# Attention on one core: both halves of a product side by side in every second step, and the two maxima matmuls of a step side by side

## The reference, cut to what matters

```
e1 = prelu(w1 @ x + b1)          # 32 x 1024 for each image
e2 = prelu(w2 @ x + b2)
asm = prelu(wa @ x + ba)         # 64 x 1024, the values
score = softmax(e1^T @ e2, axis=2)        # 1024 x 1024 for each image
out = asm @ score^T
```

## Time and profile before

| what | value |
|---|---|
| median of 3 runs | 803.87 us (802.46 to 804.47) |
| the profiled execution | 805.25 us |
| its span, first to last instruction | 803.4 us |
| TensorE matmuls busy | 690.5 us, 86% of the span |
| VectorE, GpSimd, ScalarE busy | 583.7, 424.3, 409.9 us |
| mean granted TensorE clock | 0.947 of full speed |
| attentions | from 356 to about 711 us of the span |

### The profile page before, as it was taken

The page is one execution under the profiler, slowest core; times in us unless marked ns, Lnnn a source line. Parts: engine busy times, 40 slices in busy tenths (PEclk is TensorE's granted clock), DMA queues, the critical chain, the costliest instruction groups (busy, mean ns, idle before and its releaser), DMA issues.

```text
span 803.4 us, 9141 instructions
## 1 busy us (share of the span) xinstructions
PE 690.5 (86%) x2570; PEld 350.8 (44%) x2570; DVE 583.7 (73%) x899; ACT 409.9 (51%) x709; POOL 424.3 (53%) x254
## 2 busy tenths in 40 slices
PE   4777888875499998979999999989999999866887
PEld 2332332321377775744334343333434343225883
DVE  7996999996314337876768687876868687798746
ACT  2486888984101013016464655646474656554570
POOL 5447778783512133013959587692959497632000
PEclk9898999998599999988999999999999999987899
DMA  7000000000000003032003030302102030000005
GB/s 303 0 0 1 0 0 0 0 0 1 1 0 0 0 1 78 1 79 65 14 7 74 1 80 0 80 2 52 27 11 68 0 79 1 0 1 0 1 2 209
DMA packets 8105, 24.90 MB, mean 31 GB/s; under 512 B 2048, under 2 KB 2176, under 8 KB 7936
## 3 DMA queue, kind: packets, MB, share of 16 engines
q1 hardware_dynamic: 8064, 24.45, 11.1%
HBM read 6.09 MB, written 4.19 MB: 13 GB/s over the span
## 4 chain that ended last, share of the span: by engine, by line
PE 50%; DVE 26%; issue 12%; ACT 5%; POOL 4%; DMA 1%; SPq 1%; DVEq 0%; POOLq 0%; ACTq 0%
PE PS L1415 13%; PE PS L1492 10%; PE PS L1459 7%; PE PS L1481 4%; DVE SM L625 3%; DVE RB L402 3%; PE PS L1440 3%; PE PS L1450 2%; DVE RB L477 1%; DVE PS L469 1%; PE PS L1626 1%; PE PS L1422 1%; PE PS L1654 1%; DVE RB L484 1%; DVE SM L382 1%
## 5 line engine op out<-in xcount | busy, mean ns | idle before, releaser
L625 DVE TENSOR_REDUCE SM<-PS 128x1 f32<-128x512 f32 x256 | 172.8, 686 | 80.1 <-PE PS L1459 75.7
L1006 ACT ACTIVATE RB<-PS 128x512 f32<-128x512 f32 x256 | 139.2, 599 | 107.6 <-PE PS L1481 103.4
L1231 POOL TENSOR_TENSOR RB<-RB 128x1024 f32<-128x1024 f32 x66 | 156.2, 2385 | 20.7 <-ACT RB L1006 12.3
L1459 PE MATMUL PS<-R 96*128 96x512 f32 x256 | 123.0, 481 | 12.9 <-DVE SM L625 9.2
L1415 PE MATMUL PS<-R,WS 128*128 128x512 f32 x432 | 119.7, 424 | 4.1 <-ACT R L970 4.1
L1415 PEld LDWEIGHTS PS<-R,WS 128*128 128x128 f32 x432 | 83.5, 194 | 30.7 <-issue 9.0
L1481 PE MATMUL PS<-R 98*128 98x512 f32 x256 | 87.5, 417 | 8.2 <-ACT R L1012 3.8
L1459 PEld LDWEIGHTS PS<-R 96*128 96x128 f32 x256 | 48.9, 191 | 94.1 <-issue 49.2
L1492 PE MATMUL PS<-RB 128*64 128x512 f32 x320 | 87.1, 628 | 0.0
L1354 PE MATMUL PS<-RA,W 128*128 (+1 forms) x128 | 63.1, 636 | 8.7 <-DVE RB L477 5.3
L1481 PEld LDWEIGHTS PS<-R 98*128 98x128 f32 x256 | 47.5, 192 | 36.0 <-ACT RB L1006 18.7
(11 more groups left out here) (176 smaller groups left out, 1189.9 us busy)
## 6 DMA issues: line engine op xcount, KB each, us to landing
R<-WS SPq DMA_DIRECT2D x84, 128.0 KB, 2.4
X<-x SPq DMA_DIRECT2D x8, 512.0 KB, 8.2
out<-X SPq DMA_DIRECT2D x7, 512.0 KB, 2.6
R<-R SPq DMA_DIRECT2D x24, 128.0 KB, 2.4
W<-pack SPq DMA_DIRECT2D x1, 1072.0 KB, 12.0
RB<-pack SPq DMA_DIRECT2D x1, 576.0 KB, 12.9
out<-X SPq DMA_DIRECT2D x2, 256.0 KB, 2.4
W<-pack SPq DMA_DIRECT2D x1, 201.0 KB, 3.3
```

Source lines behind the costliest of these rows:

```text
L625: v.tensor_reduce(MX[:, par, tile, h:h + 1], bank(2 + h), AX.X, ALU.max)\
L1006: act(slot[:, h * HALF:(h + 1) * HALF], bank(4 + h), ACT.Exp).then_inc(s["p_ready"], 1)
L1231: i = g.tensor_tensor(out, out, PT[j % SLOTS][par], ALU.add)
L1459: mm(bank(2 + h), stack(b, par, 0)[0:96, tile * P:(tile + 1) * P], stack(b, par, 1)[0:96, h * HALF:(h + 1) * HALF]).then_inc(s["s_mm"], 1)
```

## The change

TensorE's `attend` is reordered. Both `rows` of a step now follow `scores` at once. The products (and tails), so far one half in each step, now come as both halves in every odd step and none in an even one. `sums(p - 1, ..., 1)` moves from step 6 to step 7. Nothing changes on the other engines.

```diff
@@ -1522,10 +1522,12 @@
                     scores(p, b, n)
                     if lead:
                         rows(p + 1, (b + 1) % 3, n, 0)
-                    if n >= 4:
-                        products(p, b, n // 2 - 2, n % 2)
-                    elif lag:
-                        tail(p - 1, (b + 2) % 3, n)
+                        rows(p + 1, (b + 1) % 3, n, 1)
+                    for h in range(2 if n % 2 else 0):
+                        if n >= 4:
+                            products(p, b, n // 2 - 2, h)
+                        elif lag:
+                            tail(p - 1, (b + 2) % 3, n - 1 + h)
                     if n == 1:
                         max_rows(p, 1)
                     if n == 2 and not lead:
@@ -1533,8 +1535,8 @@
                         group(GN3A, 0, PAIRS - 2)
                     if n in (2, 3) and lead:
                         operands(p + 2, (b + 2) % 3, n - 2)
-                    if n in (5, 6) and lag:
-                        sums(p - 1, (b + 2) % 3, n - 5)
+                    if n in (5, 7) and lag:
+                        sums(p - 1, (b + 2) % 3, n // 2 - 2)
                     v0 = 7 if first else 9
                     if n in (v0, v0 + 1) and lead:
                         values(p + 1, (b + 1) % 3, n - v0)
@@ -1543,8 +1545,6 @@
                         group(GN2B, 3, PAIRS)
                     if n == 14 and lead:
                         max_rows(p + 1, 0)
-                    if lead:
-                        rows(p + 1, (b + 1) % 3, n, 1)
```

## The result

The changed kernel takes 846.2 us in the median (845.62 to 847.14, 4 runs) against 804.17 us (802.46 to 805.39, 4 runs): a ratio of 1.0525, 95% interval 1.0503 to 1.0548. The direction was forecast, the size was not: 834.0 with a range of 818 to 843. The profiled execution took 845.95 us with a span of 844.1, so 40.7 us more span than before; I had summed 30.5.

What follows compares the result with a forecast made beforehand. TensorE, busy 42.6 of 44.1 us per middle attention, was the bound; 17.1 (middle attentions) - 0.8 (first) + 5.25 (last) = +21.5, plus 9 for the clock = +30.5: 835.8 us profiled, 834.4 median, range 818 to 843.

Steps and rivals of the forecast that it cites:

- The gain: TensorE's own work per two steps falls from 4.30 to 3.94 us, 0.36 saved per pair, 2.9 per attention.
- The waits: TensorE waiting for ScalarE and VectorE in pairs without cover: 0.68 us of waits for 0.36 saved per ordinary pair.
- steps 0 and 1: Middle attention, `max_rows` behind the double product: 6.17 us against 5.62, +0.55.
- S of step 5 waits: `scores` matmul of step 5 waits about 1.8 us for exponentials behind ScalarE's second `parts` and `product_out`; steps 2 to 5 +0.77.
- S of step 8: `scores` matmul of step 8 waits 2.0 us for exponentials queued behind ScalarE's second `inverse`; steps 6 to 9 +2.57.
- steps 12 and 13: Middle attention, ordinary pair without cover: 4.62 us, +0.32 per pair.
- steps 14 and 15: Middle attention, `max_rows` in the even step: 5.1 us; steps 12 to 15 together about 9.7 against 10.40, -0.7.
- 44.06 + 2.84: Middle attention without clock falls: +2.84 us over the kernel before, +17.1 in six.
- The clock: Granted clock falls behind waits, one fall of 1.5 us per middle attention: 6 x 1.5 = 9.
- both waits dropping the clock every time: Rival: the waits of steps 5 and 8 each drop the clock, 3.0 us per attention, total 843; 15 in 100.
- The last attention: Without R, `scaled(6, 1)` comes 21.75 us after S of step 0 instead of 16.5: +5.25.
- The first attention: No tails, `sums` or `product_out`; four pairs cost +0.3, two with `values` gain: -0.8 us, give or take 1.

Runs made afterwards that it cites:

- the two pairs: Kernel before with rows side by side and products side by side only in steps 2, 3, 10 and 11: 789.7 us, ratio 0.977.
- the filler run: Changed kernel plus zero-adding matmuls behind the second sums of step 7 in the six middle attentions: 835.0 us, ratio 1.035.

## Why the forecast was right in kind and too small

*The gain.* Eight records in 1.86 us, as worked out, and where the even step has cover the saving shows: 0.38 and 0.36 us in the two pairs, 0.36 forecast. This fits the rule of the Trainium skill (TensorEngine Tiling (Array Packing), Key Properties) that a change of tiling mode drains the engine; the traces show its price alone, 0.33 us from one matmul to the next across a change of shape instead of 0.24.

*The waits.* The schedule by hand held to about a tenth of a microsecond at these points; inside them S of steps 3 and 4 came 0.3 us earlier than worked out. For a middle attention: steps 0 and 1 6.20 (forecast 6.17), S of step 5 waits, S of step 8 5.98 behind S of step 7 (5.99), steps 12 and 13 4.66 (4.62), steps 14 and 15 5.2 (5.1), the whole without falls of the clock 46.9 to 47.0 (44.06 + 2.84 = 46.9). The runs with the sums or `inverse` moved show that the wait ahead of step 8 is the dearest item. What the Trainium skill says in TensorEngine Tiling (Array Packing), PSUM Bottleneck, that tiling speeds TensorE but not the emptying of PSUM, fits the short waits of a pair without cover (S of step 1 at 1.19 us). It does not account for the wait ahead of step 8: those two runs removed it with banks and matmul shapes unchanged, so what decides there is the order in ScalarE's queue.

*The clock: the term that was mis-sized.* "I take one fall per middle attention, 6 x 1.5 = 9." The six middle attentions together are 33.3 us longer than before (301.66 against 268.33); the waits account for 6 x 2.9 = 17.4, so the clock for 16. The wait ahead of step 8 was followed by a fall in all six: step 9 took 5.1 to 7.2 us instead of the 4.5 of the filler run, in two of them because the fall lasted twice as long as the 3.3 us seen before; 9.2 us in all with what step 8 lost. The wait of step 5 was followed by one in three (5.7 us against 4.1): 4.9. The rest, about 2, lies behind the stop of the attention in which the loop turns. There the kernel before has a fall as well; it only lasts longer now:

```profile
541.50:544.80 3.30, 3.30 (x14) 1.29 (x13) 0.92 (x2) 0.59 (x2) 0.14 (x1) 0.50 0.00 0
...
555.50:565.60 10.10, 9.18 (x25) 4.22 (x25) 3.23 (x6) 2.16 (x4) 1.47 (x2) 0.50 0.00 0
```

So the count was wrong, nine new falls instead of six, and the old one at the turn grew. The price of 1.5 fits the mean of 1.6 only because sizes average out: single falls cost 0.8 to 1.7 us, the two long ones 2.5 and 2.7. The filler shows the cause of the first kind: with the same waits of the scores for ScalarE and TensorE kept busy, the clock was 1.00 through steps 8 and 9 in all six and 9.2 us came back. From one wait and one fall behind it I had treated two waits as one chance between them. Measured as the earlier trace rows measures the 1.56, they are 1.48 and 1.80 us; the longer fell every time, the shorter in three of six, and why in those three no run shows.

*The range.* 843 was the price of both waits dropping the clock every time, 18 us. The clock cost less, 16, and the time still lies above 843. Of the 11.8 us between 834.4 and 846.2, 7 are the clock in the middle attentions, 1.4 the last attention, 0.9 the work behind it, 0.4 the work ahead of the first, 0.5 the other terms, and 1.6 come from the step from the profiled execution to the median: I took 1.4 off, as the profiled execution of the kernel before lay above its median, and this time it lay 0.25 below. The range had room for the clock alone.

*The last attention.* `scaled(6, 1)` is at 728.40, 23.2 us after S of step 0 at 705.21; 21.75 was forecast, 16.5 it was before. The product of step 3 took 3.23 us there, at half clock, instead of 1.94. That is 1.3 of the missing 1.4, a fall I had not counted; in the run with `inverse` moved, which has none there, `scaled(6, 1)` is at 22.0. The wait ahead of it is no longer than the one of 0.94 us behind which the clock had stayed at 1.00, but another of 0.33 follows it:

```profile
710.81 0.73 PE L1481 MATMUL PS<-R 98*128 98x512 f32 x2 [0.94 <-ACT R L1012]
...
711.99 1.28 PE L1481 MATMUL PS<-R 98*128 98x512 f32 x2 [0.33 <-ACT RB L1006]
713.20 3.23 PE L1492 MATMUL PS<-RB,RA 128*64 128x512 f32 x8
```

Behind `scaled(6, 1)` VectorE's chain took 30.2 us to its next `scaled` instead of 29.6.

*The first attention* fell by 0.6 us (0.8 forecast), which is luck: the fall of the kernel before from 398.2 to 401.5 is not in the kernel after, whose clock is 1.00 from 371.5 to 418.5. Priced at the same 1.5 us, an estimate, that fall is more than the whole difference, so the order alone made this attention longer. The same wait is still there, 1.53 us ahead of R at 398.78, and no fall follows it.

*Rows side by side.* I had costed it at nothing. Alone it gains 7 us, and within the whole change it saves more than that, as products alone cost 27 us more. I had read the undisturbed step of the earlier trace rows, in which nothing waits, for all sixteen; in steps 6, 9, 13 and 14 of the kernel before, R or `max_rows` waits for VectorE. In step 9 it starts its product 1.26 us after S (516.86 to 518.12) with such a wait, 0.46 more than in step 10 (520.36 to 521.16) without one, and that is the whole difference in that step (3.06 against 3.51).

The sum of it: +0.4 before the attentions, -0.6, +33.3, +6.7 in the last up to `scaled(6, 1)`, +0.9 behind: 40.7.

## What to carry to other kernels

A matmul that stands between two users of the same bank is their cover. Bundling it saves a change of shape only where something else fills the gap it leaves; look for such steps one by one, and leave the others alone. When an instruction moves to a later step on one engine, look up where the engine that consumes it has queued its own call: here the consumer waited a full step in front of the next exponentials, and that was half the loss. And if a change makes new waits on TensorE that are about as long as one behind which the trace shows the clock at its lower level, price up to one fall behind each of them, not one for all, and let the range cover falls elsewhere: the length of one wait did not decide it here.

## What the runs showed of the hardware

- More work made the kernel faster: 1.8 us of matmuls by zero in six places, 846.2 to 835.0 us. 9.2 us of the difference lie right behind them, where the granted clock stayed at its upper level.
- Falls of the same kind differ in length: behind the same wait of 1.80 us the granted clock was 0.50 for 3.3 us in four attentions of the kernel after and for 6.7 us in two (from 432.6 to 439.3 and from 634.0 to 640.7), where step 9 took 6.6 and 7.2 us.
- The same wait need not have the same effect: behind 1.48 us ahead of step 5 the clock fell in three of six middle attentions. Behind 0.94 us it stayed at 1.00 in the kernel before (674.5 to 678.0); behind 0.94 and 0.33 us it fell in the last attention of the kernel after (0.50 from 712.5 to 715.8). Behind 1.56 us it fell in the first attention of the kernel before, behind 1.53 us in the same place of the kernel after it did not.
